# A row of negated maxima put into place by four small DMA transfers instead of four matrix products and a ScalarE copy

## The chip, the cores and the metric

The kernel runs on one NeuronCore of a Trainium2 chip. The metric is the device time of one execution in microseconds (us). "PE" is TensorE, "DVE" VectorE, "ACT" ScalarE, "POOL" GpSimd and "SP" SyncE, which here issues nearly all DMA transfers.

## The reference

One decoder layer on 8 rows of 512 tokens (width 512). A first attention over the 8 rows and a projection of a context are the first half. The second half, where the change lies, is this:

```python
k, v = split(src @ W_src.T + b_src); q = x @ W_tgt.T + b_tgt      # masked, 8 heads of 64
scores = q @ k.T / sqrt(64);  scores = where(src_mask == 0, -inf, scores)
attn = softmax(scores)                     # 512 x 512 for each of 8 batches and 8 heads
x = layernorm(x + cat([x, attn @ v]) @ W_out.T + b_out)
x = layernorm(x + relu(x @ w1.T + b1) @ quantized(w2).T + b2)     # width 2048
```

## The kernel before

The second half (`phase_b`) goes through 8 batches of 512 tokens. In each batch it makes the queries, then runs 8 heads. The feed-forward of the batch before is put in between: after each half head PE does one of 16 blocks of 12 matmuls (`feed_forward1`, line 1204). Batch 0 has no batch before it, so the same places hold transposes of the feed-forward's weights. Batches 1 to 6 and the last run the same order of work.

Each head needs the maximum over the keys for each of 512 queries before it can take exponentials. The scores are made twice. PE first makes them with queries on the partitions (`scores`, line 1232), DVE takes the maximum of each row (line 1576), so the maxima lie in columns: 128 partitions by 4 tiles of queries. Then PE makes the transposed scores with keys on the partitions (`transposed_scores`, lines 1249 and 1250), and there the maximum must be subtracted along the free axis. It is subtracted inside the second product: row 64 (`D2`) of `k2` is one, and row 64 of `q2` holds the negated maxima of the 512 queries.

To turn four columns into that row, the kernel before does three things for each head. DVE writes the negated maxima, as fp16, into column 64 of `mz` (line 1580). PE multiplies each of the four `mz` tiles by an identity (`maximum_row`, line 1238, 128 columns each, into bank `b_mr`). ACT copies partition 64 of that bank to `q2[D2]` (line 1408).

Each engine runs its own list in order. The order on PE within head h is: scores of head h+1 (first half), transposed scores of h (first half), `values` of head h-1 (48 small matmuls, lines 1262 to 1265), scores of h+1 (second half), a feed-forward block, transposed scores of h (second half), the row of maxima of h+1, a feed-forward block. `values` waits for `p_lo`, which DVE makes (line 1531) after ACT's exponentials and its copy `p_hi`.

SP's list for one batch of the loop issues the loads of the queries in three groups (`queries`, lines 1103 and 1104, six transfers for each group), then the load of the next rows (`load_x1`, line 1086). Then it stands at the wait of `load_heads` until the last head of the batch. The third group waits for `q_lo` of tile 3, which DVE makes after the negated maxima of head 0:

```python
                maximum(b, 0, 1)
                queries_low(b, 3)
```

The waits of one semaphore with a loop's register are kept apart from the next instruction by `stand_alone`, which increments an otherwise unused semaphore.

Of the kernel before, what the change touches and what calls it, by code (L numbers as in the profile page):

```python
# [73 lines left out]
def stand_alone(eng, sem):  # L74


    eng.sem_inc(sem, 1)
# [877 lines left out]
def phase_b(nc, ctx, d, w):  # L955
# [15 lines left out]
    rows_b = sb("rows_b", [P, E], F16)  # L971
    b2q = sb("b2q", [P, E], F16)
    b1, bt = sb("b1", [P, FT], F32), sb("bt", [P, 4], F32)
    ident16 = sb("ident16", [P, P], F16)

    x1n, x2 = w.x1n, w.q[:, 4:8, :]
    o, pf = w.k[:, 0:4, :], w.k[:, 4:8, :]
# [5 lines left out]
    k2 = sb("k2", [P, H2, B], F16)  # L983
    k1 = sb("k1", [P, H2, B], F16)
    v_hi, v_lo = sb("v_hi", [P, 4, H2, DV], F16), sb("v_lo", [P, 4, E], F16)
    mz = sb("mz", [P, 8, DV], F16)
    mrow = sb("mrow", [P, B], F32)
    mneg = sb("mneg", [P, B], F32)
    mcol = sb("mcol", [P, 4], F32)
# [25 lines left out]
    tq_b, om_b = [*st_b, mr_b, av_b], [*sx_b, *ff_b]  # L1015

    names = ("xt_filled", "xt_hi", "xt_lo", "q_filled", "q_masked", "q_hi", "q_lo", "m_made", "sx_filled", "sx_max",
             "negm", "mr_filled", "mr_copied", "st_filled", "st_exp", "p_hi", "p_lo", "av_filled", "o_rden",
             "o_norm", "x1_row_hi", "x1_row_lo", "x1_used", "ot_filled", "ot_hi", "ot_lo", "om_filled", "om_used", "x2t_filled", "x2t_hi", "x2t_lo",
             "f1_filled", "relu", "f2_filled", "f2_used", "f2_sum", "l2_stats", "l2_mv", "l2_rstd", "l2_done",  # L1020
             "l3_stats", "l3_mv", "l3_rstd", "l3_done", "m_ld", "k_ld", "v_ld",
# [25 lines left out]
    with nc.Block() as block:  # L1047
        @block.sync
        def _(sp):
# [44 lines left out]
            def queries(b, g):  # L1094
# [4 lines left out]
                for a in range(2):  # L1099
# [3 lines left out]
                        sp.dma_start(dst, qn[0][rows, tiles, :]).then_inc(qs_ld[g][a], 16)  # L1103
                    sp.dma_start(q2[0:D2, heads, :], qn[1][rows, tiles, :]).then_inc(qs_ld[g][a], 16)

            def store(b, tt):
                sp.wait_ge(s["l3_done"], 4 * b + tt + 1)
                stand_alone(sp, alone["sp"])
                sp.dma_start(out_o[b, tt], x2[:, tt, :]).then_inc(out_st[tt], 16)
# [16 lines left out]
                queries(0, g)  # L1126
            for n in range(2, 4):
                load_weights(n)
            load_x1(1, True)
            sp.wait_ge(s["wq_filled"], 4)  # L1130
            for tt in range(4):
                load_residual(0, tt, True)
            for n in range(4, FT):
                load_weights(n)
            load_heads(1, False)
            for tt in range(4):
                turn_x1(1, tt)
            with sp.Fori(0, NBATCH - 2) as b:
                for g in range(len(GROUPS)):
                    queries(b + 1, g)  # L1140
                load_x1(b + 2)
                load_heads(b + 2, False)
                for half in ((0, 1), (2, 3)):
                    for tt in half:
                        store(b, tt)
                    for tt in half:
                        turn_x1(b + 2, tt)
                    for tt in half:
                        load_residual(b + 1, tt, False)
            last = NBATCH - 1  # L1150
            for g in range(len(GROUPS)):
                queries(last, g)
            for tt in range(4):
                store(last - 1, tt)
            for tt in range(4):
# [6 lines left out]
        @block.gpsimd  # L1162
        def _(pool):

            pool.memset(v_hi[:, :, :, D2:DV], 1.0).then_inc(s["made"], 1)
            pool.tensor_copy(ident16[:, :], w.ident[:, :]).then_inc(s["made"], 1)
            pool.memset(rows_b[:, :], 0.0).then_inc(s["made"], 1)
            def norm_factors(l, b, tt):
                pool.wait_ge(s[l + "_mv"], 4 * b + tt + 1)
                i = tt + (4 if l == "l3" else 0)  # L1170
                layer_norm_factors(pool, w, mv[i], vs, rstd[i], s[l + "_rstd"], 4 * (4 * b + tt))

            def x1_rows_lo(b, tt):
                pool.wait_ge(s["x1_row_hi"], 4 * (b - 1) + tt + 1)
                stand_alone(pool, alone["act"])
                pool.tensor_tensor(x1_lo[tt], x1n[:, tt, :], x1_hi[tt][:, :], ALU.subtract).then_inc(s["x1_row_lo"], 1)  # L1176

            for tt in range(4):
                x1_rows_lo(1, tt)
            with pool.Fori(0, NBATCH - 2) as b:  # L1180
                for tt in range(4):
                    norm_factors("l2", b, tt)
                for tt in range(4):
                    x1_rows_lo(b + 2, tt)
                for tt in range(4):
                    norm_factors("l3", b, tt)
            last = NBATCH - 1
            for at in (last - 1, last):
                for l in ("l2", "l3"):
                    for tt in range(4):  # L1190
                        norm_factors(l, at, tt)

        @block.tensor
        def _(pe):
# [37 lines left out]
                    pe.matmul(sx_b[tt % 2][:, :], q1[:, h, tt * P:(tt + 1) * P], k1[:, h, :], start=True,  # L1232
                              stop=True).then_inc(s["sx_filled"], 1)

            def maximum_row(b, h):
                pe.wait_ge(s["negm"], 8 * b + h + 1)
                for tt in range(4):
                    mm = pe.matmul(mr_b[0:DV, tt * P:(tt + 1) * P], mz[:, 4 * (h % 2) + tt, :], ident16[:, :],
                                   start=True, stop=True)
                mm.then_inc(s["mr_filled"], 1)  # L1240

            def transposed_scores(b, h, half):
                for st in (2 * half, 2 * half + 1):
                    if st == 0:
                        pe.wait_ge(s["mr_copied"], 8 * b + h + 1)
                    if h or st >= 2:
                        pe.wait_ge(s["st_exp"], 32 * b + 4 * h + st - 1)
                    keys = slice(st * P, (st + 1) * P)
                    pe.matmul(st_b[st % 2][:, :], k1[:, h, keys], q1[:, h, :], start=True, stop=False)
                    pe.matmul(st_b[st % 2][:, :], k2[:, h, keys], q2[:, h, :], start=False,  # L1250
                              stop=True).then_inc(s["st_filled"], 1)
# [60 lines left out]
            def heads(b, ff):  # L1312
# [1 line left out]

                feed_forward1(ff, 0)
                pe.wait_ge(s["q_masked"], 4 * b + 4)
                maximum_row(b, 0)
                for h in range(H2):
                    for g, (i, _) in enumerate(GROUPS):
                        for a in range(2):  # L1320
                            if h + 1 == 2 * i + a:
                                pe.wait_ge(qs_ld[g][a], 48 * (b + 1))
                    if h + 1 < H2:
                        scores(b, h + 1, 0)
                    transposed_scores(b, h, 0)
                    if h == 1:
                        pe.wait_ge(s["v_ld"], 80 * (b + 1))
                    if h:
                        values(b, h - 1)
                    if h + 1 < H2:  # L1330
                        scores(b, h + 1, 1)
                    feed_forward1(ff, 2 * h + 1)
                    transposed_scores(b, h, 1)
                    if h + 1 < H2:
                        maximum_row(b, h + 1)
                        feed_forward1(ff, 2 * h + 2)
                feed_forward2(ff, 0)
                feed_forward2(ff, 1)
# [43 lines left out]
            x1_transposes()  # L1382
            pe.wait_ge(s["wq_lo"], len(jobs))
            queries_and_first_scores(0, None)
            pe.wait_ge(s["rows_made"], 3)
            pe.wait_ge(s["made"], 2)
            heads(0, None)
            with pe.Fori(0, NBATCH - 1) as b:
                output_rest(b)
# [11 lines left out]
        def _(act):  # L1401
            def hi(dst, src, filled, count, done, scale=1.0):
                act.wait_ge(filled, count)
                act.activation(dst, src, ACT.Copy, scale=scale).then_inc(done, 1)  # L1404

            def maximum_row(b, h):
                act.wait_ge(s["mr_filled"], 8 * b + h + 1)
                act.activation(q2[D2:DV, h, :], mr_b[D2:DV, :], ACT.Copy).then_inc(s["mr_copied"], 1)

            def normalize(l, b, tt):  # L1410
                act.wait_ge(s[l + "_rstd"], 4 * (4 * b + tt) + 4)
# [49 lines left out]

            def heads(b, ff, rows=True):
                relu(ff, 0)
                maximum_row(b, 0)
                for h in range(H2):
                    exponentials(b, h, 0)
                    exponentials_high(b, h, 0)
                    relu(ff, 2 * h + 1)
                    exponentials(b, h, 1)
                    if h + 1 < H2:  # L1470
                        maximum_row(b, h + 1)
                    exponentials_high(b, h, 1)
                    if h + 1 < H2:
                        relu(ff, 2 * h + 2)
# [24 lines left out]
            for i in range(4):  # L1499
                queries_hi(0, i)  # L1500
            act.wait_ge(s["cols_ld"], 32)
            act.wait_ge(s["rows_made"], 3)
            heads(0, None)
            def batch(b, rows):
                for tt in range(3):
# [22 lines left out]
        def _(dve):  # L1528
# [40 lines left out]
            def maximum(b, h, half):  # L1569
# [7 lines left out]
                                             mx[:, h % 2, tt:tt + 1]).then_inc(s["sx_max"], 1)  # L1577
                if half:
                    dve.wait_ge(s["sx_max"], 32 * b + 4 * h + 4)
                    dve.tensor_scalar(mz[:, 4 * (h % 2):4 * (h % 2) + 4, D2], mx[:, h % 2, :], -1.0, None,  # L1580
                                      ALU.mult).then_inc(s["negm"], 1)

            def exponentials_low(b, h, half):
# [81 lines left out]

            dve.memset(q2[D2:P, :, :], 0.0).then_inc(s["rows_made"], 1)
            for n, (_, high, lo) in enumerate(jobs):
                if n == 4:
                    dve.memset(mz[:, :, :], 0.0).then_inc(s["rows_made"], 1)
                if n == 8:  # L1670
                    dve.wait_ge(s["rows_made"], 2)
                    dve.tensor_scalar(k2[D2:P, :, :], q2[D2:P, :, :], w.ident[D2:P, D2:D2 + 1], None,
                                      ALU.add).then_inc(s["rows_made"], 1)
                weights_low(lo, om_b[n % 4], high, s["wq_hi"], n + 1, s["wq_lo"])
# [4 lines left out]
            dve.tensor_copy(b2q[:, :], b2_n[:, :]).then_inc(s["step"], 1)  # L1679
            dve.tensor_scalar(raw[:, :], raw[:, :], WS, None, ALU.mult).then_inc(s["step"], 1)  # L1680
            dve.wait_ge(s["step"], 3)
            dve.wait_ge(s["made"], 3)
            negated_high_rows(dve, rows_b[0:2, :], raw[:, :], s["step"])
            dve.wait_ge(s["step"], 4)
            split_rows(dve, rows_b[0:2, :], raw[:, :], w.ident[0:2, 1:2], s["step"])
# [75 lines left out]
```

## Time and profile before

| what | value |
|---|---|
| median of 3 runs | 1929.81 us (1927.22 to 1932.05) |
| the profiled execution, its own time | 1929.76 us |
| its span in the trace | 1927.9 us |
| second half, from about | 822 us to the end |
| PE busy, share of the span | 95% |
| DVE, ACT, POOL busy | 69%, 41%, 29% |

The span is what the trace covers; 1.9 us of the execution's own time lie around it. PE's busy time is modelled: one matmul of 512 columns is drawn 380 ns long, while the next starts about 215 ns after it. So a gap on PE is read from the starts of instructions.

### The profile page before, as it was taken

The page shows a single profiled execution, that of the slowest core. Times are in us where ns is not written, and L with a number is a line of the kernel's source. Part 1 is how long each engine was busy: PE and PEld are TensorE (multiplying, and loading weights), DVE is VectorE, ACT ScalarE, POOL GpSimd, SP SyncE. Part 2 cuts the span into 40 slices and gives each one's busy share as a digit, 9 for nine tenths or more (in the row PEclk, how much of TensorE's full clock was granted, in tenths as well). Part 3 has the DMA queues.
Part 4 walks back from the last instruction along what each step waited for, and adds up shares of the span by engine and source line. Part 5 has one row for each costly group of instructions (what it writes and reads, how often), then busy time and mean ns, then how long its engine had stood idle before and what let it go on. Part 6 is the DMA issues. An engine that isn't in the chain of part 4 may idle for free. (4 is left out here: it accounts for less than half of the span.)

```text
span 1927.9 us, 33302 instructions
## 1 busy us (share of the span) xinstructions
PE 1829.5 (95%) x12476; PEld 1003.3 (52%) x12476; DVE 1333.2 (69%) x1676; ACT 785.3 (41%) x1208; POOL 558.7 (29%) x576
## 2 busy tenths in 40 slices
PE   7999999999999989878899999999999999999998
PEld 3665465546554646445455454455454554554543
DVE  2899998999899998667465554655655646556521
ACT  3423222222222222248365363562653635626522
POOL 3135964786368345400102002003011020030010
PEclk9999999999999999979999999999999999999999
DMA  8436355425633566574413406207135052071010
GB/s 212 124 79 151 78 152 143 116 77 151 150 94 99 125 172 137 150 167 157 99 39 61 122 1 116 66 1 138 44 51 131 1 111 72 1 133 27 12 33 22
DMA packets 322654, 183.97 MB, mean 95 GB/s; under 512 B 225584, under 2 KB 278832, under 8 KB 322511
## 3 DMA queue, kind: packets, MB, share of 16 engines
q1 hardware_dynamic: 316448, 178.37, 38.9%
q10 hardware_dynamic: 6062, 3.49, 0.8%
q8 instruction: 114, 1.87, 0.4%
q14 instruction: 30, 0.24, 0.0%
HBM read 94.75 MB, written 33.55 MB: 67 GB/s over the span
## 5 line engine op out<-in xcount | busy, mean ns | idle before, releaser
L1531 DVE TENSOR_TENSOR p_lo<-k,p_hi 128x1024 f16<-128x1024 f32 x128 | 156.8, 1225 | 194.4 <-ACT p_hi L1404 194.4
L1176 POOL TENSOR_TENSOR q<-q,x_hi 128x512 f16<-128x512 f32 x28 | 37.6, 1374 | 638.7 <-ACT x_hi L1457 638.7
L1576 DVE CUSTOM_DVE_ANT_0 junk<-b_sx,mneg 128x512 f16<-128x512 f32 x256 | 175.9, 687 | 32.6 <-issue 23.2
L1204 PE MATMUL b_ff<-x2T_hi,w1T_hi 128*128 128x512 f16 x512 | 194.7, 380 | 1.9 <-DVE x2T_lo L1531 1.9
L1204 PE MATMUL b_ff<-x2T_lo,w1T_hi 128*128 128x512 f16 x512 | 194.7, 380 | 0.0
L1204 PE MATMUL b_ff<-x2T_hi,w1T_lo 128*128 128x512 f16 x512 | 194.6, 380 | 0.0
L1436 ACT ACTIVATE k<-b_st,mbias 128x512 f32<-128x512 f32 x256 | 161.9, 685 | 14.0 <-PE b_st L1250 13.4
L577 PE MATMUL sm_b<-cT_hi,wsT_hi 128*128 128x256 f16 x512 | 141.8, 277 | 15.2 <-DMA cT_lo<-rows_lo 13.6
L784 DVE TENSOR_TENSOR prod<-q,k 128x4096 f32<-128x4096 f32 x32 | 142.2, 4443 | 17.5 <-ACT q L660 16.7
L1404 ACT ACTIVATE p_hi<-k 128x1024 f16<-128x1024 f32 x128 | 135.3, 1057 | 45.5 <-PE b_av L1265 43.1
L1428 ACT ACTIVATE hq<-b_ff,b 128x512 fp8e4<-128x512 f32 x128 | 88.0, 687 | 155.6 <-PE b_ff L1204 149.0
L543 PE MATMUL pj_b<-winT_hi,xT_hi 128*128 128x512 f16 x384 | 146.8, 382 | 0.9 <-DVE winT_lo L851 0.9
L543 PE MATMUL pj_b<-winT_lo,xT_hi 128*128 128x512 f16 x384 | 146.8, 382 | 0.0
L543 PE MATMUL pj_b<-winT_hi,xT_lo 128*128 128x512 f16 x384 | 146.5, 382 | 0.0
L824 DVE TENSOR_TENSOR prod<-pr,v 128x4096 f32<-128x4096 f32 x32 | 142.4, 4451 | 1.1
L577 PE MATMUL sm_b<-cT_hi,wsT_lo 128*128 128x256 f16 x512 | 141.7, 277 | 0.0
L577 PE MATMUL sm_b<-cT_lo,wsT_hi 128*128 128x256 f16 x512 | 141.7, 277 | 0.0
L789 DVE TENSOR_REDUCE pr<-prod 128x128 f32<-128x4096 f32 x32 | 141.1, 4410 | 0.1
L1413 ACT ACTIVATE q<-q,rstdb 128x512 f32<-128x512 f32 x64 | 52.2, 815 | 216.4 <-POOL rstdb L88 216.3
L440 POOL TENSOR_TENSOR rows_lo<-cn,rows_hi 128x512 f16<-128x512 f32 x64 | 117.0, 1835 | 61.0 <-ACT rows_hi L644 60.9
L1204 PE MATMUL b_ff<-w2T,hq 128*128 128x512 fp8e4 x512 | 112.9, 379 | 1.6 <-ACT hq L1428 1.0
L82 POOL TENSOR_TENSOR vsb<-mvb,consts 128x1 f32<-128x1 f32 x64 | 14.9, 233 | 337.6 <-DVE mvb L1546 337.6
(272 smaller groups left out, 4368.9 us busy)
## 6 DMA issues: line engine op xcount, KB each, us to landing
cn<-in_ctx_dram SPq DMA_DIRECT2D x64, 256.0 KB, 3.1
k<-kT_scratch SPq DMA_DIRECT2D x24, 512.0 KB, 7.7
x<-in_x_dram SPq DMA_DIRECT2D x32, 256.0 KB, 3.1
x_scratch<-x SPq DMA_DIRECT2D x32, 256.0 KB, 2.2
q<-x_scratch SPq DMA_DIRECT2D x8, 1024.0 KB, 5.6
q<-x_scratch SPq DMA_DIRECT2D x32, 256.0 KB, 2.9
out_dram<-q SPq DMA_DIRECT2D x32, 256.0 KB, 4.4
xn<-in_x_dram SPq DMA_DIRECT2D x24, 256.0 KB, 2.9
```

Of the source, the lines that this page charges most:

```text
L440: pool.tensor_tensor(lo[:, :], row_source(kind, i), hi[:, :], ALU.subtract).then_inc(s["row_lo"], 1)
L543: pe.matmul(out, a, c, start=(j == 0 and m == 0), stop=False)
L577: pe.matmul(dst, a, z, start=(j == 0 and m == 0), stop=False)
L784: dve.tensor_tensor(prod[:, :, :], q[:, t, :].unsqueeze(1).to_broadcast([P, T, E]), k[:, :, :], ALU.mult).then_inc(s["sc_prod"], 1)
L789: dve.tensor_reduce(pr[:, t].rearrange("p h s -> p s h"), prod[:, :, :].rearrange("p s (h d) -> p s h d", h=H1), AX.X, ALU.add).then_inc(s ...
L824: dve.tensor_tensor(by_head(prod), probs, by_head(v), ALU.mult).then_inc(s["av_prod"], 1)
L1204: mm = pe.matmul(out, a, c, start=(start and n == 0), stop=end)
L1404: act.activation(dst, src, ACT.Copy, scale=scale).then_inc(done, 1)
L1428: act.activation(hq[:, f, :], ff_b[f % 2][:, :], ACT.Relu, bias=b1[:, f:f + 1], scale=1.0 / WS, saturate=False).then_inc(s["relu"], 1)
L1436: act.activation(pf[:, st, :], st_b[st % 2][:, :], ACT.Exp, bias=mbias[:, st:st + 1], scale=D2 ** -0.5).then_inc(s["st_exp"], 1)
L1531: dve.tensor_tensor(dst, bank, hi, ALU.subtract).then_inc(out, 1)
L1576: dve.tensor_tensor_reduce(junk[:, :], sx_b[tt % 2][:, :], mneg[:, :], 1.0, NEG, ALU.add, ALU.max, mx[:, h % 2, tt:tt + 1]).then_inc(s["sx ...
```

## The change

The negated maxima are written to a small tile `least` (two slots by head), and SP moves each of its four columns to its 128 elements of the row `q2[D2, h]` with a DMA transfer of 128 elements of two bytes. PE's four matmuls, the identity in fp16, the tile `mz` and ACT's copy are gone. PE waits for the four transfers (`row_ld`) where it waited for the copy. On SP the transfers of head 0 come after the three groups of queries and ahead of `load_x1`; those of heads 1 to 7 come behind `load_x1`. In batch 0 they stand between the loads of weights, and those of head 0 stand behind the loads of weight blocks 2 and 3.

```diff
+            def maximum_row(b, h):                                     # on SP
+                sp.wait_ge(s["negm"], 8 * b + h + 1)
+                stand_alone(sp, alone["sp"])
+                with nc.allow_non_contiguous_dma(reason="a column as a row"):
+                    for tt in range(4):
+                        sp.dma_start(q2[D2:DV, h, tt * P:(tt + 1) * P], least[:, h % 2, tt:tt + 1]).then_inc(
+                            s["row_ld"], 16)
...
             for n in range(2, 4):
                 load_weights(n)
+            maximum_row(0, 0)
             load_x1(1, True)
...
-            for n in range(4, FT):
-                load_weights(n)
+            for h in range(1, H2):
+                for n in range(2 * h + 2, 2 * h + 4) if h < 7 else ():
+                    load_weights(n)
+                maximum_row(0, h)
...
             with sp.Fori(0, NBATCH - 2) as b:
                 for g in range(len(GROUPS)):
                     queries(b + 1, g)
+                maximum_row(b + 1, 0)
                 load_x1(b + 2)
+                for h in range(1, H2):
+                    maximum_row(b + 1, h)
                 load_heads(b + 2, False)
...
-            def maximum_row(b, h):                                     # on PE
-                pe.wait_ge(s["negm"], 8 * b + h + 1)
-                for tt in range(4):
-                    mm = pe.matmul(mr_b[0:DV, tt * P:(tt + 1) * P], mz[:, 4 * (h % 2) + tt, :], ident16[:, :],
-                                   start=True, stop=True)
-                mm.then_inc(s["mr_filled"], 1)
...
                     if st == 0:
-                        pe.wait_ge(s["mr_copied"], 8 * b + h + 1)
+                        pe.wait_ge(s["row_ld"], 512 * b + 64 * h + 64)
+                        stand_alone(pe, alone["pe"])
...
-            def maximum_row(b, h):                                     # on ACT
-                act.wait_ge(s["mr_filled"], 8 * b + h + 1)
-                act.activation(q2[D2:DV, h, :], mr_b[D2:DV, :], ACT.Copy).then_inc(s["mr_copied"], 1)
...
-                    dve.tensor_scalar(mz[:, 4 * (h % 2):4 * (h % 2) + 4, D2], mx[:, h % 2, :], -1.0, None,
+                    dve.tensor_scalar(least[:, h % 2, :], mx[:, h % 2, :], -1.0, None,
                                       ALU.mult).then_inc(s["negm"], 1)
```

## Rows read from the trace of the kernel before

**Rows 1.** The page: busy time, share and instructions of each engine.
```profile
PE 1829.5 (95%) x12476; PEld 1003.3 (52%) x12476; DVE 1333.2 (69%) x1676; ACT 785.3 (41%) x1208; POOL 558.7 (29%) x576
```

**Rows 2.** Busy time by stretch, batch 3: PE, PEld, DVE, ACT, POOL, granted clock, DMA share, GB/s.
```profile
1184.00:1303.00 119.00, 117.08 (x861) 59.72 (x860) 66.25 (x139) 65.16 (x94) 8.16 (x25) 1.00 0.26 59
```

**Rows 3.** Timeline of all engines, batch 3, heads 5 and 6: start, length, engine, line.
```profile
1278.15 0.18 DVE L1580 TENSOR_SCALAR mz<-mxb 128x4 f16<-128x4 f32 x1
...
1279.68 0.39 PE L1238 MATMUL b_mr<-ident,mz 128*65 128x128 f16 x4
...
1279.90 0.38 PE L1204 MATMUL b_ff<-x2T_hi,w1T_hi 128*128 128x512 f16 x1
...
1280.97 0.59 ACT L1408 ACTIVATE q<-b_mr 1x512 f16<-1x512 f32 x1
...
1282.68 1.23 DVE L1531 TENSOR_TENSOR p_lo<-k,p_hi 128x1024 f16<-128x1024 f32 x1 [3.20 <-ACT p_hi L1404]
...
1282.93 0.38 PE L1249 MATMUL b_st<-q,k 128*128 128x512 f16 x1
...
1283.57 0.38 PE L1250 MATMUL b_st<-q,k 128*128 128x512 f16 x1
...
1283.96 0.20 PE L1262 MATMUL b_av<-v_hi,p_hi 128*128 128x65 f16 x1
```

**Rows 4.** DMA issues: out<-in, queue, count, size of each, median us from issue to landing.
```profile
b<-in_b_dram ACTq DMA_DIRECT2D x1, 8.0 KB, 4.1
...
q<-qn_lo SPq DMA_DIRECT2D x32, 64.0 KB, 2.0
...
small<-in_mask_dram SPq DMA_DIRECT2D x16, 1.0 KB, 2.7
...
mcol<-in_mask_dram SPq DMA_DIRECT2D x8, 2.0 KB, 4.3
```

**Rows 5.** By tile, the mask columns: ns that one issue holds SP, min/median/max.
```profile
L1057 SPq DMA_DIRECT2D mcol<-in_mask_dram x8: 372/383/435, 822.6 to 1690.7; - x8
...
L336 SPq DMA_DIRECT2D small<-in_mask_dram x16: 428/434/582, 15.5 to 774.5; - x16
```

**Rows 6.** Timeline of all engines, batch 3, start of head 0.
```profile
1225.07 0.18 DVE L1580 TENSOR_SCALAR mz<-mxb 128x4 f16<-128x4 f32 x1
1225.14 0.68 DVE L1531 TENSOR_TENSOR qn_lo<-qf,qn_hi 128x512 f16<-128x512 f32 x1
...
1225.92 1.30 SPq L1103 DMA_DIRECT2D q<-qn_hi  x2
...
1226.80 0.39 PE L1249 MATMUL b_st<-q,k 128*128 128x512 f16 x1 [0.66 <-ACT q L1408]
...
1229.24 0.61 SPq L1104 DMA_DIRECT2D q<-qn_lo  x1
```

**Rows 7.** Busy time by stretch, batch 0; columns as in rows 2.
```profile
860.00:862.00 2.00, 0.41 (x3) 0.41 (x4) 0.15 (x1) 1.95 (x3) 0.00 (x0) 0.95 0.83 272
862.00:864.00 2.00, 1.15 (x6) 0.75 (x5) 1.88 (x2) 0.61 (x2) 0.00 (x0) 0.50 0.61 152
...
868.00:870.00 2.00, 2.00 (x39) 1.80 (x37) 0.64 (x3) 0.68 (x1) 0.00 (x0) 0.85 1.07 410
```

**Rows 8.** Timeline of all engines, batch 0, heads 0 and 1.
```profile
854.51 0.39 PE L1249 MATMUL b_st<-q,k 128*128 128x512 f16 x1 [0.25 <-ACT q L1408]
...
860.34 0.43 SPq L1118 DMA_DIRECT2D hq<-in_w_dram  x1
...
861.59 0.98 PE L1197 MATMUL b_ff<-ident,x2T_lo 128*128 128x128 f32 x4 [1.97 <-DMA x2T_lo<-in_w_dram]
```

**Rows 9.** Timeline of all engines, batch 0, between heads 3 and 4.
```profile
887.39 0.37 SPq L1118 DMA_DIRECT2D hq<-in_w_dram  x1
...
888.11 0.18 DVE L1580 TENSOR_SCALAR mz<-mxb 128x4 f16<-128x4 f32 x1
...
891.04 0.38 PE L1249 MATMUL b_st<-q,k 128*128 128x512 f16 x1
```

More of the change, by code:

```diff
@@ L973, in phase_b @@
     b1, bt = sb("b1", [P, FT], F32), sb("bt", [P, 4], F32)
-    ident16 = sb("ident16", [P, P], F16)
     x1n, x2 = w.x1n, w.q[:, 4:8, :]
@@ L985, in phase_b @@
     v_hi, v_lo = sb("v_hi", [P, 4, H2, DV], F16), sb("v_lo", [P, 4, E], F16)
-    mz = sb("mz", [P, 8, DV], F16)
+    least = sb("least", [P, 2, 4], F16)
     mrow = sb("mrow", [P, B], F32)
@@ L1017, in phase_b @@
     names = ("xt_filled", "xt_hi", "xt_lo", "q_filled", "q_masked", "q_hi", "q_lo", "m_made", "sx_filled", "sx_max",
-             "negm", "mr_filled", "mr_copied", "st_filled", "st_exp", "p_hi", "p_lo", "av_filled", "o_rden",
+             "negm", "row_ld", "st_filled", "st_exp", "p_hi", "p_lo", "av_filled", "o_rden",
              "o_norm", "x1_row_hi", "x1_row_lo", "x1_used", "ot_filled", "ot_hi", "ot_lo", "om_filled", "om_used", "x2t_filled", "x2t_hi", "x2t_lo",
@@ L1152, in _ @@
                 queries(last, g)
+            for h in range(H2):
+                maximum_row(last, h)
             for tt in range(4):
@@ L1165, in _ @@
             pool.memset(v_hi[:, :, :, D2:DV], 1.0).then_inc(s["made"], 1)
-            pool.tensor_copy(ident16[:, :], w.ident[:, :]).then_inc(s["made"], 1)
             pool.memset(rows_b[:, :], 0.0).then_inc(s["made"], 1)
@@ L1316, in heads @@
                 pe.wait_ge(s["q_masked"], 4 * b + 4)
-                maximum_row(b, 0)
                 for h in range(H2):
@@ L1334, in heads @@
                     if h + 1 < H2:
-                        maximum_row(b, h + 1)
                         feed_forward1(ff, 2 * h + 2)
@@ L1384, in _ @@
             queries_and_first_scores(0, None)
-            pe.wait_ge(s["rows_made"], 3)
-            pe.wait_ge(s["made"], 2)
+            pe.wait_ge(s["rows_made"], 2)
             heads(0, None)
@@ L1463, in heads @@
                 relu(ff, 0)
-                maximum_row(b, 0)
                 for h in range(H2):
@@ L1469, in heads @@
                     exponentials(b, h, 1)
-                    if h + 1 < H2:
-                        maximum_row(b, h + 1)
                     exponentials_high(b, h, 1)
@@ L1501, in _ @@
             act.wait_ge(s["cols_ld"], 32)
-            act.wait_ge(s["rows_made"], 3)
+            act.wait_ge(s["rows_made"], 2)
             heads(0, None)
@@ L1667, in _ @@
             for n, (_, high, lo) in enumerate(jobs):
-                if n == 4:
-                    dve.memset(mz[:, :, :], 0.0).then_inc(s["rows_made"], 1)
                 if n == 8:
-                    dve.wait_ge(s["rows_made"], 2)
+                    dve.wait_ge(s["rows_made"], 1)
                     dve.tensor_scalar(k2[D2:P, :, :], q2[D2:P, :, :], w.ident[D2:P, D2:D2 + 1], None,
@@ L1681, in _ @@
             dve.wait_ge(s["step"], 3)
-            dve.wait_ge(s["made"], 3)
+            dve.wait_ge(s["made"], 2)
             negated_high_rows(dve, rows_b[0:2, :], raw[:, :], s["step"])
```

## The prediction

> **What bounds the kernel now.** I read the page first: PE is busy for 95% of the span, DVE for 69%, ACT for 41% [rows 1]. The second question is whether this also holds in the stage that is changed. In the stretch with batch 3's heads PE is busy for 117 of 119 us at the full granted clock of 1.00 [rows 2]. So work taken from ACT or DVE is worth nothing by itself there; only what PE does, and what PE waits for, counts.
>
> Third, the timeline of one head, read by the starts of PE's instructions [rows 3]. The negated maxima are ready at 1278.33 (1278.15 + 0.18). PE reaches the four matmuls at 1279.68 and is at the feed-forward block at 1279.90: they hold PE for 0.22 us and don't wait. The transposed scores that need the row start at 1282.93. Three matmuls later it is 1283.57, so one takes (1283.57 - 1282.93) / 3 = 0.21, PE is free at 1283.78, and `values` starts at 1283.96: PE idles for 0.18 us, because `p_lo` ends at 1283.91. This pattern stands in heads 2 to 6 of batches 1 to 7, 35 times, within 0.15 us; head 1 reads much the same, and in head 7 the idle time is about 0.6.
>
> Fourth, SP's list around head 0 of a batch [rows 6]. There the negated maxima are ready at 1225.25, PE needs the row at once (1226.80, after waiting 0.66 for ACT's copy), and SP is just starting six issues that end at 1229.24 + 0.61 = 1229.85. The same is so in all seven batches 1 to 7: the issues end 3.0 us behind PE's start each time.
>
> **The change part by part.** *Removed from PE:* 0.22 us for each head. *Removed from ACT:* the 0.59 us copy [rows 3]. It stands ahead of `p_hi`, thus ahead of `p_lo`, so `p_lo` comes 0.59 earlier, and the 0.18 of idle time ahead of `values` goes too. A head whose row comes in time so gains 0.22 + 0.18 = 0.40 us; head 7 gains up to 0.59, the whole copy. For a batch that is 6 x 0.40 + 0.59 = 3.0 us, for seven batches 21 us. The DVE instruction writes the same 128x4 elements to another tile: nothing.
>
> *Added: four transfers for each head.* The trace shows none like them (128 elements of two bytes, SBUF to one partition). For the issue the nearest rows are the mask columns, also element by element: 0.38 and 0.43 us [rows 5]; the six query issues of 3.93 us give 0.65 as the upper end [rows 6]. I take 0.48 with the step between issues, as the columns are nearer. For landing, 64 KB from SBUF to SBUF take 2.0 us, a mask column of 256 elements 2.7, one of 512 elements behind another transfer 4.3, and 2048 elements of a bias 4.1 [rows 4]. So an element adds little, and the floor is about 2.0. I take 2.2 for 128 elements; 2.0 and 2.7 are the ends, with 4.3 for a rival. SP wakes 0.10 us after its event (1225.82 to 1225.92 in rows 6). From the negated maxima to the last landing: 0.10 + 3 x 0.48 + 2.2 = 3.7 us, ends 0.10 + 3 x 0.38 + 2.0 = 3.2 and 0.10 + 3 x 0.65 + 2.7 = 4.8.
>
> *Cover in heads 1 to 7.* From 1278.33 to 1282.93 are 4.60 us, less the 0.22 that PE is now earlier: 4.38 [rows 3]. 3.7 fits, 0.7 to spare; the upper end would stall PE by 0.4 for each head, which just eats the gain. Behind the new wait of SP stand only the loads for later batches, which waited for the end of the heads before too; `load_x1`, moved behind head 0's row, has 60 us.
>
> *Head 0 of batches 1 to 7.* SP comes to the row only at 1229.85, although the maxima have been there for 4.6 us. The four issues and the landing end at 1229.85 + 3.7 = 1233.6, where PE started at 1226.80 before [rows 6]: 6.8 us later, ends 6.3 and 7.9. Nothing hides it: PE's list is in order, and the feed-forward block and `values` stand behind the wait. Seven times: +48 us.
>
> *The clock after it.* PE idles for about 7.5 us there. In batch 0 a wait of 1.97 us [rows 8] is followed by a granted clock of 0.50, the lower of the two levels, from 862 on; it is mixed again (0.85) in 868 to 870 [rows 7], though PE was busy meanwhile. I take 4.5 us at half clock behind each stall, which loses half of that, 2.2 us, with 0 and 3 as ends: 7 x 2.2 = +15 us.
>
> *Batch 0, head 0.* The row now stands behind the four loads of weights that end at 860.34 + 0.43 [rows 8], and lands about 4.5 us later, at 865.3, where PE started at 854.51: 10.8 us. Some of it returns, since PE waited for those weights anyway (1.97 and more). I take 7 for heads 0 and 1.
>
> *Batch 0, heads 2 to 7.* The cover is only from 888.29 to 891.04, 2.75 us, and 512 KB of weights have just been issued [rows 9]. 3.7 less 2.75 and some queueing is 1.3 us a head: 6 x 1.3 = 8. Batch 0 in all: +15, ends 8 and 28.
>
> *Sum:* 48 + 15 - 21 + 15 = +57 us. The profiled execution's own time is 1929.8 (span 1927.9 and 1.9 around it), which equals the median of the runs: 1987 us.
>
> **The rivals.** *(a) Small elements land slowly.* If a transfer takes the 4.3 us of the longest mask column [rows 4], the row needs 5.8 us and PE stalls in every head: 5.8 - 4.38 - 0.40 = 1.0 us slower for each of 49 heads than before (+50), head 0 8.9 for seven (+62), clock +15, batch 0 about +32: 2089 us. Against it speaks the bias of 2048 elements in 4.1. The Trainium skill speaks for it ("DMA: Bandwidth & Descriptors", sections "Rules for kernel authors" and "Specifications"): a last dimension that isn't contiguous becomes one descriptor per element, and pieces under 512 bytes are read, changed and written back. By that rule 128 descriptors of two bytes are the worst case; rows 4 agree on the direction (2.7 us for 1 KB against 2.0 for 64 KB), not on a large price.
>
> *(b) The clock does not fall* in the stalls, or only shortly: 1987 - 15 = 1972 us. The batch 0 rows speak against it, but there PE was also less busy around the wait.
>
> *(c) Faster.* The one mechanism is that head 0's row is not late, as when SP's six issues were done sooner or the row went ahead of them. Then the 21 us of the heads stay. It decides at 3.0 us for a batch, the gain of the other heads: the row would have to be there by 1226.80 + 3.0 = 1229.80, before SP has ended the issue of the queries. With the row fully hidden and batch 0 unchanged it would be 1909 us. Rows 6 speak against it plainly: the order of SP's list is fixed, and the six issues took 3.93 us.
>
> **How the numbers follow.** The forecast, head 0 late with a fall of the clock and rows in time elsewhere, has 0.62; (a) 0.15, (b) 0.15, (c) 0.08, half of it so small that nothing can be measured. Lower ends: 7 x 6.3 + 0 - 21 + 8 = +31, 1961. Upper ends: 7 x 7.9 + 7 x 3 + 0 + 28 = +104, 2034. The range from 1950 to 2050 holds the forecast, (b) and the milder part of (a), and leaves out (c) and the worse part of (a). A change of under 0.3%, 5.8 us, can hardly be told from none here. Slower by more: 0.92, within: 0.04, faster: 0.04.
>
> **What the profile after would show.** Right: in batches 1 to 7 PE's first line 1249 of each batch waits some 7 us for a DMA into `q`, and the granted clock is 0.50 for a few us behind it; in heads 1 to 7 no such wait, a period shorter by 0.4, and no idle time ahead of `values`; SP starts the row's issues right behind the last query issue; a row issue holds SP for 0.4 to 0.5 and lands in 2.0 to 2.7. Wrong: waits for the row in every head (a), a clock of 1.00 behind the stall (b), or a row of head 0 that lands before 1229.8 on this scale (c). If PE's waits in head 0 are there but the total has not grown, something in the batch must have given the time back, and I see nothing that could.

## The result and the profile after

The changed kernel takes 2253.89 us (median of 4 runs, 2251.01 to 2254.87), the kernel before 1930.93 beside it (4 runs, 1927.22 to 1932.59). The ratio is 1.1673, interval 1.1652 to 1.1694. I forecast 1987 us within 1950 to 2050: the direction was right, the size was not (+323 us instead of +57). The profiled execution has a span of 2252.1 us where that of before had 1927.9, so 324.2 us are to be found.

The page of the changed kernel: the engines; the granted clock in tenths, in 40 slices; and the group of transposed scores (count, then busy and mean ns, then the idle time of PE ahead of it and what ended it).

```profile
PE 1892.7 (84%) x12220; PEld 1024.5 (45%) x12220; DVE 1333.4 (59%) x1675; ACT 752.7 (33%) x1144; POOL 562.3 (25%) x575
...
PEclk9999999999999987798898898898898898898899
...
L1257 PE MATMUL b_st<-q,k 128*128 128x512 f16 x256 | 119.9, 468 | 272.9 <-DMA q<-least 272.9
```

PE is at 84% where it was at 95% [rows 1], although it has 256 instructions fewer. It stands idle for 272.9 us ahead of this one line, each time for the row. And the granted clock, which in the kernel before is under 0.9 in only one of the 40 slices, is at 0.7 to 0.9 in the second half.

The waits, and then the answer by tile for `least` (issue time in ns; at the end the time from issue to landing):

```profile
PE b_st L1257 <- DMA q<-least: 272.9, 64, 15.7
```

```profile
L1110 SPq DMA_DIRECT2D q<-least x256: 468/601/1871, 860.3 to 2126.9; - x128
...
DMA to landing us min/median/max: 2.7/4.9/7.1
```

PE waits in all 64 heads, not in head 0 and batch 0 alone. An issue holds SP for 0.60 us, and a transfer lands in 4.9, where I had taken 0.48 and 2.2. The same view for the four transfers of one undisturbed head (batch 4, head 1), in three windows: the first transfer, the second and third, the fourth.

```profile
L1110 SPq DMA_DIRECT2D q<-least x1: 469/469/469, 1543.2 to 1543.2; - x1
...
DMA to landing us min/median/max: 2.8/2.8/2.8
...
DMA to landing us min/median/max: 4.1/4.5/5.0
...
L1110 SPq DMA_DIRECT2D q<-least x1: 601/601/601, 1545.0 to 1545.0; - x1
...
DMA to landing us min/median/max: 5.5/5.5/5.5
```

Each of four equal transfers takes longer than the one ahead of it: 2.8, 4.1, 5.0, 5.5 us. (They share one semaphore, and the view gives its landings out in the order of issue.) They are issued 0.6 us apart and land 1.2 to 1.8 us apart, so they queue behind each other somewhere. The last one lands at 1545.0 + 5.5 = 1550.5, 7.4 us after the maxima (1543.11).

The timeline, heads 2 to 5 of batch 3, then heads 0 and 4 of batch 4: the starts of PE's first transposed scores, with the wait ahead of them, and the maxima.

```profile
1395.85 0.38 PE L1257 MATMUL b_st<-q,k 128*128 128x512 f16 x1 [3.02 <-DMA q<-least]
1408.26 0.59 PE L1257 MATMUL b_st<-q,k 128*128 128x512 f16 x1 [3.02 <-DMA q<-least]
1422.16 0.59 PE L1257 MATMUL b_st<-q,k 128*128 128x512 f16 x1 [2.92 <-DMA q<-least]
1435.96 0.59 PE L1257 MATMUL b_st<-q,k 128*128 128x512 f16 x1 [2.94 <-DMA q<-least]
...
1526.32 0.17 DVE L1578 TENSOR_SCALAR least<-mxb 128x4 f16<-128x4 f32 x1
...
1531.32 2.47 SPq L1110 DMA_DIRECT2D q<-least  x4
...
1538.82 0.59 PE L1257 MATMUL b_st<-q,k 128*128 128x512 f16 x1 [11.82 <-DMA q<-least]
...
1581.69 0.17 DVE L1578 TENSOR_SCALAR least<-mxb 128x4 f16<-128x4 f32 x1
...
1589.42 0.59 PE L1257 MATMUL b_st<-q,k 128*128 128x512 f16 x1 [3.02 <-DMA q<-least]
```

Head 4: maxima at 1581.86, PE starts at 1589.42, 7.56 us later; before it was 4.60 [rows 3]. Head 0: maxima at 1526.49, SP issues at 1531.32, PE starts 12.33 us after the maxima, against 1.55 before [rows 6]. From head to head it is 12.41 us once (1395.85 to 1408.26), then 13.90 and 13.80; before it was 9.62. The wait is the same 3 us each time, so the 1.4 us by which the later heads are longer are something else. The windows show it (columns as in rows 2), the first while one row has still to land, the others around the wait of another head:

```profile
1549.00:1550.00 1.00, 0.69 (x4) 0.10 (x1) 1.00 (x1) 0.62 (x1) 0.00 (x0) 1.00 0.00 0
1587.00:1590.00 3.00, 0.58 (x2) 0.29 (x3) 1.29 (x4) 0.00 (x0) 0.00 (x0) 0.86 0.00 0
1590.00:1593.00 3.00, 3.00 (x45) 2.22 (x43) 0.00 (x0) 1.37 (x2) 0.00 (x0) 0.57 0.02 5
1593.00:1596.00 3.00, 3.00 (x26) 1.49 (x23) 2.34 (x8) 1.06 (x1) 0.00 (x0) 1.00 0.00 0
```

After the 3 us of idling PE runs for some 3 us near the lower level (0.57 granted), then at the full one. And in 1549 to 1550, while one row has still to land, the DMA engines show no activity at all (0.00): what holds the row up is not drawn as a packet.

Where the 324.2 us lie, by the starts of PE's first transposed scores:

| where | before | after | gain or loss |
|---|---|---|---|
| batch 0: its head 0 | 854.51 | 869.45 | +14.9 |
| batch 0: its heads, to the next batch's head 0 (less that row's 10.8) | 113.8 | 155.1 | +41.3 |
| head 0 of batches 1 to 7, maxima to PE | 1.55 | 12.35 | 7 x 10.8 = +76 |
| batches 1 to 7, from head 0's start to head 7's (the figures are batch 2's) | 65.3 | 91.9 | 7 x 26.6 = +186 |
| rest | | | +6 |

### The profile page after: what moved, and what is told of

Its sections match the earlier page's. It is cut to its first block and busy times, and to the rows that moved or that the text cites. A ratio compares the mean times of both kernels' runs of the same rounds, so it can differ in the third digit from the quotient of the medians.

```text
span 2252.1 us, 33107 instructions
## 1 busy us (share of the span) xinstructions
PE 1892.7 (84%) x12220; PEld 1024.5 (45%) x12220; DVE 1333.4 (59%) x1675; ACT 752.7 (33%) x1144; POOL 562.3 (25%) x575
## 5 line engine op out<-in xcount | busy, mean ns | idle before, releaser
L1257 PE MATMUL b_st<-q,k 128*128 128x512 f16 x256 | 119.9, 468 | 272.9 <-DMA q<-least 272.9
L1437 ACT ACTIVATE k<-b_st,mbias 128x512 f32<-128x512 f32 x256 | 167.0, 685 | 316.8 <-PE b_st L1258 314.0
L1218 PE MATMUL b_ff<-x2T_hi,w1T_hi 128*128 128x512 f16 x512 | 199.3, 389 | 2.2 <-DVE x2T_lo L1529 2.2
L1257 PEld LDWEIGHTS b_st<-q,k 128*128 128x128 f16 x256 | 27.8, 109 | 331.6 <-issue 315.7
L1590 DVE RECIPROCAL rden<-b_av 128x4 f32<-128x4 f32 x64 | 11.7, 183 | 279.4 <-PE b_av L1273 279.4
L440 POOL TENSOR_TENSOR rows_lo<-cn,rows_hi 128x512 f16<-128x512 f32 x64 | 123.9, 1941 | 61.0 <-ACT rows_hi L644 61.0
```

Source lines behind the costliest of these rows:

```text
L440: pool.tensor_tensor(lo[:, :], row_source(kind, i), hi[:, :], ALU.subtract).then_inc(s["row_lo"], 1)
L1218: mm = pe.matmul(out, a, c, start=(start and n == 0), stop=end)
L1437: act.activation(pf[:, st, :], st_b[st % 2][:, :], ACT.Exp, bias=mbias[:, st:st + 1], scale=D2 ** -0.5).then_inc(s["st_exp"], 1)
```

## The experiments

The theory after the result: the pieces of two bytes land slowly because of what they are (their width or the one partition that they go into); everything else follows from the late row. The rivals: a transfer has a large fixed cost whatever its shape, or pieces are slow wherever they go.

**e1_shapes.** The kernel before, with small transfers that nobody reads added on SP behind the maxima of each head of batches 1 to 6; one shape for each head.

```diff
+ 1: [(da_row[D2:DV, cut(tt)], src_c[:, tt:tt + 1]) for tt in range(4)],            # the change's shape
+ 2: [(db_one[D2:DV, :], src_c[:, :])],                                             # one transfer, 128 x 8 bytes
+ 3: [(dc_far[D2 + 16 * tt:DV + 16 * tt, :], src_c[:, tt:tt + 1]) for tt in range(4)],
+ 4: [(dd_near[D2 + tt:DV + tt, :], src_c[:, tt:tt + 1]) for tt in range(4)],
+ 5: [(de_col[:, tt:tt + 1], src_c[:, tt:tt + 1]) for tt in range(4)],              # column to column
+ 6: [(df_back[:, tt:tt + 1], src_r[D2:DV, :]) for tt in range(4)],                 # row to column
+ 7: [(dg_half[D2:DV, tt * 64:tt * 64 + 64], src_c[0:64, tt:tt + 1]) for tt in range(4)]
...
```

> The kernel before, which computes all it did, with transfers added that nobody reads: in heads 1 to 7 of batches 1 to 6 SP waits for the negated maxima, issues one kind of small transfer from scratch tiles and waits for it to land. Head 1: four columns of 128 elements of two bytes into one row (da_row), as in the changed kernel. Head 2: one transfer of 128 runs of 8 bytes into one row (db_one). Head 3: four columns into four partitions 16 apart (dc_far). Head 4: into four neighbouring partitions (dd_near). Head 5: column to column, 128 partitions on either side (de_col). Head 6: one row to four columns (df_back). Head 7: four half columns of 64 elements into one row (dg_half). Theory: writes of two bytes into one partition go one after the other, about 12 ns each, so transfers of one head queue behind each other. It expects da_row to land 2.8 to 5.5 us after issue, as in the changed kernel; dc_far, de_col and df_back without a queue, all within 2.0 to 3.2; dd_near either like dc_far (the partition is the limit) or like da_row (a port shared by neighbours is); dg_half at most about 3.2; db_one about 2.8. Rival one, each transfer has a fixed cost that the next can't overlap: every kind of four shows 2.8 to 5.5, dg_half too, db_one 2.8. Rival two, a piece of two bytes is slow wherever it goes: de_col and df_back show 2.8 to 5.5 too. The time should stay within 0.3% of the kernel before.

The time was 1936.07 us in one run, beside 1934.88 for the kernel before, so the probes cost the kernel next to nothing. DMA issues of that run (columns as in rows 4):

```profile
da_row<-src_c SPq DMA_DIRECT2D x24, 0.2 KB, 7.3
dc_far<-src_c SPq DMA_DIRECT2D x24, 0.2 KB, 2.9
dd_near<-src_c SPq DMA_DIRECT2D x24, 0.2 KB, 4.5
de_col<-src_c SPq DMA_DIRECT2D x24, 0.2 KB, 1.8
df_back<-src_r SPq DMA_DIRECT2D x24, 0.2 KB, 2.0
dg_half<-src_c SPq DMA_DIRECT2D x24, 0.1 KB, 2.4
db_one<-src_c SPq DMA_DIRECT2D x6, 1.0 KB, 1.9
```

Both rivals fall. Transfers of 128 two-byte pieces into 128 partitions land in 1.8 and 2.0, so a transfer has no large fixed cost and a small piece is not slow as such. Only the column that becomes a row is slow, and less so with 64 pieces (2.4). Four neighbouring partitions are as slow as one (4.5), four that lie 16 apart are not (2.9). The first row of the list also stands behind `load_x1`, which falls into head 1, and is not to be compared. One thing was not expected: one transfer with the same 128 pieces, but of eight bytes, landed in 1.9, faster than one column of two bytes. That led to e5.

**e2_far_rows.** The four transfers go to partitions 64, 80, 96 and 112 of `q2` instead of one row; `k2` has ones in all four, so the product subtracts the same maxima.

```diff
-  sp.dma_start(q2[D2:DV, h, tt * P:(tt + 1) * P], least[:, h % 2, tt:tt + 1]).then_inc(
+  sp.dma_start(q2[D2 + 16 * tt:DV + 16 * tt, h, tt * P:(tt + 1) * P], least[:, h % 2, tt:tt + 1]).then_inc(
...
```

> The changed kernel, but the four pieces of the row go to four partitions 16 apart (64, 80, 96, 112 of q2, with ones in the same rows of k2); the product sums them, so the same result is computed. Theory (writes into one partition queue): the row is there 0.1 + 3 x 0.62 + 2.8 = 4.8 us after the maxima instead of 7.5, PE waits 0.4 us in place of 3.0 in heads 1 to 7 and the clock holds there: 49 heads x about 3.9 and 8 heads x 2.7 less, near 2040 us. Both rivals (fixed cost of each transfer; slow pieces anywhere): no change from 2254 us.

It took 2058.63 us (2056.33 to 2060.93), ratio 1.0642 (1.0608 to 1.0675). Its waits:

```profile
PE b_st L1257 <- DMA q<-least: 130.7, 57, 13.3
```

The landing is 3.0 us in the median instead of 4.9. With nothing but the destination's partition changed, 195 of the 323 us are gone. (The changed kernel itself was timed beside other runs of the kernel before; taken by the ratios, e2, e3 and e4 are 199, 31 and 63 us under it.) In batches 1 to 7 the waits are down from 3 us to 0.6 or 0.7 in heads 2 to 6, 1.1 to 1.4 in head 7 and almost none in head 1, and the granted clock no longer falls in them (1.00 in 1320 to 1330, head 2 of batch 3). The theory holds that the four transfers hinder each other in the partition that they share.

**e3_row0_ahead.** SP issues head 0's row ahead of the third group of queries.

```diff
   for g in range(len(GROUPS)):
+      if g == 2:
+          maximum_row(b + 1, 0)
       queries(b + 1, g)
-  maximum_row(b + 1, 0)
...
```

> The changed kernel with the row of head 0 ahead of the third group of queries on SP (in batch 0 ahead of that and of two loads of weights). If head 0's extra delay is SP's order, its row is there 7.5 us after the maxima instead of 12.3, and the time falls by 4.8 us for each of 7 batches and by some 8 in batch 0: about 2212 us. If the order is not what delays it (the row queues behind the query transfers anyway, or the queries moved back by 2.5 us stop PE in later heads), no change or slower than 2254.

It took 2227.54 us (2226.85 to 2228.23), ratio 1.1515 (1.1482 to 1.1548): 26 us less, not 42. Timeline of batch 4, heads 0 to 3:

```profile
1514.10 0.17 DVE L1582 TENSOR_SCALAR least<-mxb 128x4 f16<-128x4 f32 x1
...
1521.91 0.59 PE L1261 MATMUL b_st<-q,k 128*128 128x512 f16 x1 [7.13 <-DMA q<-least]
...
1533.81 0.38 PE L1261 MATMUL b_st<-q,k 128*128 128x512 f16 x1 [1.98 <-DMA q<-least]
...
1546.19 0.38 PE L1261 MATMUL b_st<-q,k 128*128 128x512 f16 x1 [2.99 <-DMA q<-least]
...
1560.15 0.59 PE L1261 MATMUL b_st<-q,k 128*128 128x512 f16 x1 [2.99 <-DMA q<-least]
```

Head 0's row now comes 7.64 us after the maxima (1514.27 to 1521.91) instead of 12.33, as expected; in seven batches that is 33 us. Head 1 waits 1.98 where it waited 0.97 in the changed kernel, but it comes no later for that: 11.90 us after head 0, against 11.84 (1538.82 to 1550.66). Two other things take from the gain. In most batches the clock now falls a head earlier: from head 2 to head 3 it is 13.96 us here (0.57 granted in 1546 to 1549) and 12.41 in the changed kernel, some 6 us in all. And batch 0 gains nothing: head 1's row stands behind loads of weights there, and PE waits 12.90 us for it.

**e4_fill.** Matmuls whose result nobody reads are put ahead of PE's wait, to see what the clock costs.

```diff
                   if st == 0:
+                      for _ in range(48 if h == 0 else 12):
+                          pe.matmul(mr_b[:, :], k1[:, 0, 0:P], q1[:, 0, :], start=True, stop=True)
                       pe.wait_ge(s["row_ld"], 512 * b + 64 * h + 64)
```

> The changed kernel with matmuls of no use put ahead of PE's wait for the row (48 in head 0, 12 in heads 1 to 7, 512 columns each, into a free bank), which fit into the time that PE idles there. Theory: the idle time lets the granted clock fall to half, and that costs about 1.4 us in most heads (period 13.8 against 12.4) and some 2 in head 0. With the idle time filled the clock stays at 1.00, the waits end where they did, and the time falls by 40 to 70 us, to about 2200. Rival: the longer periods come from something else (ACT, DVE or SP's queue): no change, or slower by the matmuls that don't fit.

It took 2194.97 us (2190.88 to 2199.07), ratio 1.1347 (1.1293 to 1.14). PE does more and the kernel is 59 us faster. The page's granted clock, and the timeline of three heads in a row:

```profile
PEclk9999999999999998899999999999999999999999
```

```profile
1405.47 0.38 PE L1259 MATMUL b_st<-q,k 128*128 128x512 f16 x1 [0.34 <-DMA q<-least]
...
1417.82 0.38 PE L1259 MATMUL b_st<-q,k 128*128 128x512 f16 x1 [0.37 <-DMA q<-least]
...
1430.18 0.38 PE L1259 MATMUL b_st<-q,k 128*128 128x512 f16 x1 [0.41 <-DMA q<-least]
```

The row comes no earlier, PE's idle time is filled, and the period is a steady 12.35 us instead of 13.8. So of the changed kernel's 323 us some 264 are late rows and some 59 a clock that falls where PE idles.

**e5_widths.** Two unread transfers of one kind for each head, in the kernel before.

```diff
+ 2: [(row(cut(tt)), src_c[:, tt:tt + 1]) for tt in range(2)],                                # 2 bytes
+ 3: [(row(slice(256 * tt, 256 * tt + 256)), src_c[:, 2 * tt:2 * tt + 2]) for tt in range(2)],# 4 bytes
+ 4: [(row(slice(512 * tt, 512 * tt + 512)), src_c[:, :]) for tt in range(2)],                # 8 bytes
+ 5: [(row(slice(512 * tt, 512 * tt + 512, 4)), src_c[:, tt:tt + 1]) for tt in range(2)],     # 2 bytes, 8 apart
+ 6: [(row(cut(tt), 4 * tt), src_c[:, tt:tt + 1]) for tt in range(2)],                        # partitions 64, 68
+ 7: [(row(cut(tt), 2 * tt), src_c[:, tt:tt + 1]) for tt in range(2)]                         # partitions 64, 66
...
```

> The kernel before, which computes all it did, with two transfers at a time added in heads 1 to 7 of batches 1 to 6, that nobody reads. Each is 128 pieces from 128 partitions; what differs is where and how wide they are written. Head 1 and head 2: two bytes, next to each other in partition 64 (head 1 behind the load of the next rows). Head 3: four bytes. Head 4: eight bytes. Head 5: two bytes, but 8 bytes apart in partition 64. Head 6: two bytes, partitions 64 and 68. Head 7: two bytes, partitions 64 and 66. The first shapes showed two-byte pieces into one partition landing after 2.8 us and more, eight-byte pieces after 1.9. Theory A, a write of two bytes is slow by its width: head 5 like head 2 (2.8, then about 4.1), head 4 about 1.9 and 1.9, head 3 tells whether four bytes are wide enough. Theory B, writes that touch the same few bytes wait for each other: head 5 fast (1.9 to 2.2). Theory C, the eight-byte transfer was fast only since nothing stood behind it: head 4's second lands after 2.5 or more. If groups of four neighbouring partitions share the limit, head 6 shows 2.8 for both and head 7 2.8, then about 4.1.

The time was 1929.91 us. The landings by tile, for one batch, heads 2 to 7 one after the other (head 1 stands behind `load_x1` again):

```profile
DMA to landing us min/median/max: 2.8/3.3/3.8
...
DMA to landing us min/median/max: 1.9/1.9/2.0
...
DMA to landing us min/median/max: 1.9/1.9/2.0
...
DMA to landing us min/median/max: 2.6/2.8/3.1
...
DMA to landing us min/median/max: 2.6/2.8/3.0
...
DMA to landing us min/median/max: 2.8/3.3/3.8
```

In heads 2 to 4 the number of pieces, the partitions they come from and the partition they go to are the same; only the width differs. Two bytes: 2.8 and 3.8. Four bytes: 1.9 and 2.0. Eight: the same 1.9 and 2.0. So a single transfer is slow by the width of two bytes; with its pieces set eight bytes apart it still takes 2.6. The delay of the second transfer is another matter: eight bytes apart it lands in 3.1, nearly as with partitions 64 and 68 (3.0), although both transfers go into partition 64. So the queue needs, besides the width, pieces that lie next to each other; theories A and B each hold for a part. Partitions 64 and 66 hinder each other as one partition does (3.8), 64 and 68 hardly (3.0). The Trainium skill ("SBUF — State Buffer", section "Door 1: The DMA port swizzle") says that four neighbouring partitions share one port of the memory and the next four have another; these rows agree with that grouping.

**e6_one_move.** The row is moved by one transfer of 128 pieces of eight bytes. It then holds the four tiles interleaved, so `scores` takes every fourth query for a tile instead of 128 in a row.

```diff
-  for tt in range(4):
-      sp.dma_start(q2[D2:DV, h, tt * P:(tt + 1) * P], least[:, h % 2, tt:tt + 1]).then_inc(s["row_ld"], 16)
+  sp.dma_start(q2[D2:DV, h, :], least[:, h % 2, :]).then_inc(s["row_ld"], 16)
...
-  pe.matmul(sx_b[tt % 2][:, :], q1[:, h, tt * P:(tt + 1) * P], k1[:, h, :], ...
+  pe.matmul(sx_b[tt % 2][:, :], q1[:, h, :].rearrange("d (p t) -> d t p", t=4)[:, tt, :], k1[:, h, :], ...
...
```

> The changed kernel with one transfer for each head: 128 pieces of 8 bytes, partition p's four values next to each other in the row. So that the row stands in the order of the queries, PE's first scores take every fourth query (columns tt, tt + 4, ...) in place of 128 neighbours; the result is the same. If width and number of the pieces were the whole of the trouble in heads 1 to 7, the row is there 0.1 + 1.9 us after the maxima, PE doesn't wait in heads 1 to 7, and each gains 0.4 us on the kernel before; head 0 still stands behind the query transfers: 5 us later than before and 2 for the clock, in 7 batches, and some 8 in batch 0. About 1970 us against 1935 before. Rival: PE's loads of every fourth column are slow (256 of them): each 0.1 us of that adds 26 us. If the number of transfers matters only by SP's issue time, heads 1 to 7 would still wait some, about 2100.

It took 1966.65 us (1964.27 to 1970.42), ratio 1.018 (1.0158 to 1.0202). Timeline of head 0 of batch 3, and the windows behind it (columns as in rows 2), with the waits of the whole run ahead of them:

```profile
1242.88 0.17 DVE L1576 TENSOR_SCALAR least<-mxb 128x4 f16<-128x4 f32 x1
...
1247.94 0.54 SPq L1109 DMA_DIRECT2D q<-least  x1
...
1250.01 0.58 PE L1255 MATMUL b_st<-q,k 128*128 128x512 f16 x1 [6.43 <-DMA q<-least]
```

```profile
PE b_st L1255 <- DMA q<-least: 59.5, 10, 11.5
```

```profile
1250.00:1252.00 2.00, 1.99 (x5) 0.71 (x6) 0.00 (x0) 0.77 (x2) 0.00 (x0) 0.50 0.74 213
1252.00:1254.00 2.00, 2.00 (x7) 0.74 (x6) 1.31 (x3) 1.66 (x2) 0.00 (x0) 0.59 0.79 308
```

This kernel behaves as my prediction described: no wait in heads 1 to 7 of batches 1 to 7 (the ten waits are head 0 of the eight batches and two heads of batch 0), a late row in head 0, and the clock at the lower level (0.50) behind it. It came out 20 us under the 1987 that I forecast. A late row costs 6.96 - 1.55 = 5.4 us of latency, and the head behind it is 1.8 us longer by the clock (9.54 from head 0 to head 1, against 7.77 in e8, where head 0 waits only 1.6).

**e7_one_move_ahead.** e6 with head 0's row ahead of the third query group, as in e3.

> As e6_one_move, and the row of head 0 ahead of the third group of queries on SP. Head 0's row then comes about 2.1 us after the maxima against 1.56 before, so each batch loses 0.6 there and gains 3.0 in heads 1 to 7: 7 x 2.4 = 17 us, and batch 0 about 2. About 1916 us against 1935 before, ratio 0.990. If the copy's 0.59 us ahead of p_lo was hidden after all, only the 0.22 of the matmuls stays: about 1927. If loads of every fourth column are slow: slower than before.

It took 1929.6 us (12 runs, 1925.82 to 1939.31), ratio 0.9987 (0.9974 to 1.0): no difference that can be told. Timeline: head 1 of batch 3 (the load, the row, PE), then heads 5 and 6, and head 5 of the kernel before (its head 6 is in rows 3).

```profile
1233.14 0.40 SPq L1085 DMA_DIRECT2D q<-x_scratch  x1
...
1233.74 0.54 SPq L1109 DMA_DIRECT2D q<-least  x1
...
1238.98 0.38 PE L1259 MATMUL b_st<-q,k 128*128 128x512 f16 x1 [1.09 <-DMA q<-least]
...
1275.90 0.38 PE L1259 MATMUL b_st<-q,k 128*128 128x512 f16 x1
...
1285.11 0.38 PE L1259 MATMUL b_st<-q,k 128*128 128x512 f16 x1
```

```profile
1273.32 0.38 PE L1249 MATMUL b_st<-q,k 128*128 128x512 f16 x1
```

The heads are 9.21 us apart (1275.90 to 1285.11), 0.40 less than before (1273.32 to 1282.93): the gain that I had worked out for a row in time is there. It is given back mostly where a row stands behind a load: head 1's row is issued 0.6 us after the 1 MB of `load_x1` and keeps PE waiting for 1.1 to 1.5 us in batches 1 to 6, and in batch 0, behind the weights, for 11.46 once. Head 0 also starts 0.6 us later than before in each batch (2.15 us after the maxima).

**e8_loads_behind.** e7 with those loads moved: `load_x1` behind head 1's row, and in batch 0 most of the loads that stood ahead of a row behind it.

```diff
...
-  load_x1(b + 2)
-  for h in range(1, H2):
+  maximum_row(b + 1, 1)
+  load_x1(b + 2)
+  for h in range(2, H2):
       maximum_row(b + 1, h)
...
```

> As e7_one_move_ahead, with the loads that stood ahead of rows of head 1 moved behind them: in the loop the load of the next rows behind the row of head 1; in batch 0 the loads of the next rows and of the residual behind the rows of heads 2 and 3, and the loads of two weight blocks behind each row. The heads 2 to 6 of e7 already had the period that the prediction gave them (9.22 against 9.62 before), but head 1's row waited 1.1 to 1.6 us in batches 1 to 6 and 11.5 us in batch 0, behind those loads. If that is where e7's gain went, the time falls by 6 x 1.3 and by about 8 in batch 0: about 1914 us, ratio 0.991 to the kernel before. If the loads moved back stop somebody else (PE for weights in batch 0, ACT for the next rows), no better than e7, 1930.

It took 1909.98 us (6 runs, 1908.61 to 1921.8), ratio 0.9893 (0.9873 to 0.9913): faster than both kernels, than the one before by 1.1%. Its waits:

```profile
PE b_st L1262 <- DMA q<-least: 15.8, 11, 1.9
```

Of the 272.9 us of waiting for the row 15.8 are left. The idea of the change, a row moved by DMA instead of by PE, is worth some 20 us once the pieces are wide and the row goes ahead of the loads.

## Why the prediction was wrong, step by step

**The step that failed** is the landing: "So an element adds little, and the floor is about 2.0. I take 2.2 for 128 elements". Measured were 2.8 for the first transfer of a head and 5.5 for the fourth, which is the one that PE waits for. The rows from which I took it, the mask columns and the biases [rows 4], are pieces of four bytes or more; the mask columns and the bias go into 128 partitions. None of them is a piece of two bytes into one partition. e1 and e5 show that each of those two properties by itself lands in 1.8 to 2.0 us, and that only both together are slow. I also took four transfers as independent, with the last landing 2.2 us after its issue; in fact they queue. The issue was mis-sized too, 0.60 instead of 0.48, which adds 3 x 0.12 = 0.4. Landing and issue together are 3.7 of the 3.9 us by which the 7.56 exceed my 3.7; the rest is PE's own start after the landing (1550.5 to 1550.66), which I had left out.

**Cover in heads 1 to 7.** The cover itself was right: in e6, where the row is in time, PE starts 4.39 us after the maxima. The measured latency of 7.56 us against the cover of 4.38 makes a wait of 3.2 (shown: 3.0) in place of none. By my own sum that is 7.56 - 4.38 - 0.40 = 2.8 us a head, 49 x 2.8 = 136 us. Measured were 186. The other 50 are nearly all the clock, which I had counted only behind head 0, and which falls behind the waits of 3 us too. e4, with the idle time filled, takes 85.4 us (1198.34 to 1283.76) for the stretch of batch 2 that takes 91.9 in the changed kernel and 65.3 before, so 7 x 6.5 = 45 are the clock and 7 x 20.1 = 141 the late rows.

**Rival (a)** was this mechanism, with the right sign for every term, but 5.8 us of latency instead of 7.56 and no clock behind heads 1 to 7: 2089 us. It had 0.15, and the upper end of the range, 2050, left its worse part out. The rule that I set beside it, of the Trainium skill ("DMA: Bandwidth & Descriptors", "Rules for kernel authors" and "Specifications"), pointed the right way here, but not to the cause: pieces of four and eight bytes are under its 512 too, and landed like 64 KB do (1.9 against 2.0). The same page of the Trainium skill, section "Why small descriptors are slow (HBM only)", says that transfers from SBUF to SBUF do not suffer the penalty it describes, with packets of 128 bytes as its example; two-byte pieces into one partition were dear here all the same (2.8 us against 1.9 for four bytes).

**Head 0 of batches 1 to 7.** That SP reaches the row only behind the six query issues was right (1531.32, with the last query issue ending at 1531.10). The row came 10.8 us later than before instead of 6.8, the difference being the landing again. With a fast landing it is 5.4 (e6).

**The clock.** It falls behind head 0 as forecast; I took 2.2 us each time, and e6 measured 1.8. Rival (b), a clock that holds, is out.

**Batch 0** cost 56 us instead of 15: PE waits for the row in all of its heads, 15.7 us in head 0 and 4.7 to 6.0 in the others.

**The gain of 0.40 us a head** was right (e7: 9.21 against 9.62), and the sum of +57 for rows that land fast was near: e6, where they do, measured 1966.65 - 1931.77 = +35. Of the difference of 22, 10 are head 0 (5.4 for 6.8, seven times), 3 the clock, and what is left, some 9, is mostly batch 0 (8 us measured in e6, 15 forecast). **Rival (c)**, faster, needed head 0's row ahead of the queries; it takes that and the order of the loads (e7, e8), and ends at 1910 where I had 1909. That the two agree so closely is in part luck: e8 also moves the row in one transfer of wide pieces, and its head 0 still loses 0.6 us in each batch.

**Still open** is what inside the chip makes writes of two bytes into one partition slow. The packets are over while the row still lands (0.00 of DMA share from 1546.5 on, the last landing at 1550.5), so the time lies behind what the trace draws. Nothing here tells a limit of the port from one of the memory behind it. Head 5 of e5 speaks against a plain limit that all two-byte writes into a partition share, since its second transfer was hardly held up; pieces four bytes apart were not run.

## What to carry to other kernels

A price for a small DMA is read from a row with the same piece width and the same destination partitions; rows with both of them other were off by a factor of 2.5 here (2.2 taken, 5.5 measured for the last of four). Where a column must become a row, pack it so that one piece is at least four bytes, with one transfer for all of it: that landed in 1.9 us here. A transfer that takes the place of work on an engine also inherits the order of its queue: put it ahead of the loads that nobody waits for yet, and count the clock that PE loses behind every new wait, not only behind the long one.

## What the runs showed of the hardware that I had not expected

- Two-byte pieces into one partition land in 2.8 us for 128 of them and further transfers queue behind (5.5 for the fourth); four-byte pieces in 1.9, eight-byte pieces in 1.9.
- Transfers into four neighbouring partitions queue in the same way (4.5 us median for 64 to 67); into partitions 4 or 16 apart they hardly do (3.0 at most for two, 2.9 median for four). Nor do they with the pieces eight bytes apart in one partition (2.6 and 3.1).
- Behind PE's wait of 3 us the granted clock was near its lower level for some 3 us (0.57 in 1590 to 1593), in most heads, though not in all of the first ones of a batch; matmuls without any use, put into the waits (12 a head, 48 in head 0), made the kernel 59 us faster.
- Taking every fourth column as stationary operand lengthened a weight load from 98 to 113 ns, which stayed hidden behind the matmuls.
